# Layer 1's cross attention: scores in five rotating PSUM banks, one bank for the turned probabilities, a loop over 20 batches

## The reference, cut to what matters

```python
B, N, C = x1.shape              # 128, 32, 128
M = x2.shape[1]                 # 257
H, D = (NUM_HEADS, HEAD_DIM)    # 16, 8
q = (x1 @ Wq.T).reshape(B, N, H, D).transpose(0, 2, 1, 3)
k = (x2 @ Wk.T).reshape(B, M, H, D).transpose(0, 2, 1, 3)
v = (x2 @ Wv.T).reshape(B, M, H, D).transpose(0, 2, 1, 3)
q = _layernorm(q, ln_g, ln_b)
k = _layernorm(k, ln_g, ln_b)
q = q * SCALE
attn = jnp.einsum('bhnd,bhmd->bhnm', q, k)
attn = jax.nn.softmax(attn, axis=-1)
out = jnp.einsum('bhnm,bhmd->bhnd', attn, v)
out = out.transpose(0, 2, 1, 3).reshape(B, N, C)
return out @ Wp.T + bp
```

## Time and profile before

| | us |
|---|---|
| median of 3 runs (lowest to highest) | 3743.85 (3743.23 to 3745.98) |
| the profiled execution's own time | 3772.4 |
| its span, first to last instruction | 3770.2 |
| PE busy, share of the span | 2981.6 (79%) |
| DVE busy | 2481.5 (66%) |
| ACT busy | 2041.2 (54%) |
| POOL busy | 1973.8 (52%) |
| first to last `l1x_att_pS` matmul group, start | 802.0 to 1222.4 |

### The profile page before, as it was taken

One profiled execution on the slowest core, in us unless ns is written; L12 is line 12 of the kernel. 1 busy time (PEld: TensorE's weight loads), 2 busy tenths in 40 slices (PEclk: granted clock), 3 DMA queues, 4 the chain that ended last, 5 costly groups with the idle time before them and its releaser, 6 DMA issues. The chain is left out here.

```text
span 3770.2 us, 79125 instructions
## 1 busy us (share of the span) xinstructions
PE 2981.6 (79%) x23619; PEld 2060.2 (55%) x23619; DVE 2481.5 (66%) x6661; ACT 2041.2 (54%) x6345; POOL 1973.8 (52%) x1964
## 2 busy tenths in 40 slices
PE   6989596779999697575999996787862668968967
PEld 5769434446666585453677773333322436735645
DVE  7966676658888573333788885898985123447863
ACT  5545405658888454223677774555530125549954
POOL 5630205767777793053566664888870541117830
PEclk9989798989999798788899998998985778968979
DMA  3300001322222000111111112444431229800000
GB/s 102 91 26 0 6 1 60 101 68 81 79 80 76 8 1 6 59 37 42 41 36 36 36 35 103 135 141 135 146 107 60 31 41 232 199 7 1 2 7 22
DMA packets 142430, 233.64 MB, mean 62 GB/s; under 512 B 28796, under 2 KB 104862, under 8 KB 141575
## 3 DMA queue, kind: packets, MB, share of 16 engines
q1 hardware_dynamic: 134088, 221.61, 20.1%
q0 software_dynamic: 8128, 9.45, 1.4%
HBM read 200.44 MB, written 13.71 MB: 57 GB/s over the span
## 5 line engine op out<-in xcount | busy, mean ns | idle before, releaser
L3208 PE MATMUL l2a_pY<-l2a_hc,ident 128*128 128x512 f32 x512 | 273.4, 673 | 91.3 <-POOL l2a_hc L3127 56.9
L2446 POOL TENSOR_TENSOR l2x_att_prob<-l2x_att_prob,l2x_att_rs 128x1024 f32<-128x1024 f32 x128 | 242.5, 1895 | 148.3 <-DVE l2x_att_rs L2677 148.3
L3097 POOL TENSOR_TENSOR l2a_dbu<-l2a_dx,l2a_BC 128x1024 f32<-128x1024 f32 x128 | 298.7, 2355 | 20.8 <-PE l2a_pY L3208 10.6
L2446 POOL TENSOR_TENSOR l1x_att_prob<-l1x_att_prob,l1x_att_rs 128x1024 f32<-128x1024 f32 x128 | 242.6, 1895 | 106.9 <-DVE l1x_att_rs L2677 106.9
L2634 ACT ACTIVATE l2x_att_prob<-l2x_att_pS,l2x_att_nmx 128x257 f32<-128x257 f32 x512 | 236.4, 475 | 94.5 <-DVE l2x_att_nmx L2672 94.5
L3225 ACT ACTIVATE l2a_pA<-l2a_dl,l2a_A 128x512 f32<-128x512 f32 x256 | 174.7, 690 | 187.7 <-DVE l2a_pH L3331 112.5
L2634 ACT ACTIVATE l1x_att_prob<-l1x_att_pS,l1x_att_nmx 128x257 f32<-128x257 f32 x512 | 236.4, 475 | 72.9 <-DVE l1x_att_nmx L2672 72.8
L3208 PEld LDWEIGHTS l2a_pY<-l2a_hc,ident 128*128 128x128 f32 x512 | 103.6, 211 | 252.8 <-issue 119.4
L2672 DVE TENSOR_REDUCE l1x_att_nmx<-l1x_att_pS 128x1 f32<-128x257 f32 x512 | 182.0, 418 | 89.2 <-PE l1x_att_pS L2545 89.2
L3331 DVE TENSOR_TENSOR_SCAN l2a_pH<-l2a_pA,l2a_dbu 128x512 f32<-128x512 f32 x192 | 224.9, 1217 | 23.5 <-POOL l2a_dbu L3097 12.3
L2672 DVE TENSOR_REDUCE l2x_att_nmx<-l2x_att_pS 128x1 f32<-128x257 f32 x512 | 182.0, 418 | 53.4 <-PE l2x_att_pS L2550 53.4
(11 more groups left out here) (741 smaller groups left out, 9086.4 us busy)
## 6 DMA issues: line engine op xcount, KB each, us to landing
l2a_BC<-l2a_rows SPq DMA_DIRECT2D x128, 512.0 KB, 3.8
l3x_att_ctn<-ctx_n SPq DMA_DIRECT2D x32, 576.0 KB, 12.4
l0x_att_kvs<-ctx_t SPq DMA_DIRECT2D x32, 514.0 KB, 3.6
l1x_k_xin<-ctx_t SPq DMA_DIRECT2D x32, 514.0 KB, 3.5
l1x_att_ctx<-ctx_t SPq DMA_DIRECT2D x128, 128.5 KB, 2.1
l1x_att_kT<-l1x_KA SPq DMA_DIRECT2D x128, 128.5 KB, 2.2
l2x_att_ctx<-ctx_t SPq DMA_DIRECT2D x128, 128.5 KB, 2.1
l3x_att_ctx<-ctx_t SPq DMA_DIRECT2D x32, 514.0 KB, 10.7
```

Of the source, the lines that this page charges most:

```text
L2446: pool.tensor_tensor(p, p, bc(rs[:, b, :], 2, LAST), ALU.mult).then_inc(scaled, 1)
L3097: pool.tensor_tensor(dbu[:, u % 3], dx[:, g % 2], bc(BC[:, u % RING, 0, :], 1, NC), ALU.mult).then_inc(dbu_made, 1)
L3208: last = pe.matmul(pY[c][:, :], env.ident[:, :], hc[:, u % 3, c, :], start=False, stop=n == NS - 1)
```

## The change

For the call with `KA`, `pS` has five banks and `pT` one. Scores of batch t (counted modulo 5) go to banks (4t + j) modulo 5, and so maxima and exponentials read them there. PE's scores wait for a new semaphore `third_read`, counted by the third exponential of the batch before, in place of `p_made`. Both halves of a turn use the one bank: half 0 waits for ACT's copy of the batch before, half 1 for DVE's copy of half 0 of the same batch, and half 1 is issued after `values(n+2)` and no longer before it. PE, ACT and DVE run `run_slots20`, whose loop body is 20 slots (6 passes), since bank numbers must be constants and repeat after five batches and buffers after four. POOL and SP keep `run_slots4`. DVE's and ACT's orders within a slot stay. With `KA=None` everything stays.

```diff
+def run_slots20(eng, slot, units, first, last):
+    low, high = 4, units - 4
+    for n in range(first, low):
+        slot(n, n % 4, n // 4, n % 5)
+    with eng.Fori(0, (high - low) // 20) as i:
+        for c in range(20):
+            slot(20 * i + low + c, c % 4, 5 * i + (low + c) // 4, (low + c) % 5)
+    for n in range(high, units + last):
+        slot(n, n % 4, n // 4, n % 5)
...
-        pS = st.ps("pS", [P, R, 512])
-        pT = [st.ps(f"pT{j}", [P, 512]) for j in range(2)]
+        BANKS = 5 if KA is not None else R
+        pS = st.ps("pS", [P, BANKS, 512])
+        pT = [st.ps(f"pT{j}", [P, 512]) for j in range(2 if KA is None else 1)]
...
+        def bank(t, j):
+            return (R * t + j) % BANKS
+        turns = run_slots4 if KA is None else run_slots20
...
-                    after(pe, p_made, n - 1)
+                    after(pe, p_made if KA is None else third_read, n - 1)
...
-                        last = pe.matmul(pS[:, j, 0:KEYS], ...
+                        last = pe.matmul(pS[:, bank(t, j), 0:KEYS], ...
...
                 def turn(n, b, h):
                     if h == 0:
                         pe.wait_ge(scaled, made(n))
-                        after(pe, t_kept_d, n - 1)
+                        after(pe, t_kept_d if KA is None else t_kept_a, n - 1)
+                    elif KA is None:
+                        after(pe, t_kept_a, n - 1)
                     else:
-                        after(pe, t_kept_a, n - 1)
+                        pe.wait_ge(t_kept_d, made(n))
                     for j in range(R):
-                        last = pe.transpose(pT[h][:, j * P:(j + 1) * P], ...
+                        last = pe.transpose(pT[h % len(pT)][:, j * P:(j + 1) * P], ...
...
                     if inside(n - 1):
                         turn(n - 1, (c - 1) % 4, 0)
-                        turn(n - 1, (c - 1) % 4, 1)
+                        if KA is None:
+                            turn(n - 1, (c - 1) % 4, 1)
...
                     if inside(n + 2):
                         values(n + 2, c, k)
-                run_slots4(pe, slot, B, -2, 3)
+                    if inside(n - 1) and KA is not None:
+                        turn(n - 1, (c - 1) % 4, 1)
+                turns(pe, slot, B, -2, 3)
...
+                        if j == 2 and KA is not None:
+                            last.then_inc(third_read, 1)
                     last.then_inc(p_made, 1)
...
-                    act.activation(probT[:, b % 2, 1, :], pT[1][:, :], ACT.Copy).then_inc(t_kept_a, 1)
+                    act.activation(probT[:, b % 2, 1, :], pT[-1][:, :], ACT.Copy).then_inc(t_kept_a, 1)
...
-                run_slots4(act, slot, B, -2, 3)
+                turns(act, slot, B, -2, 3)
...
-                run_slots4(dve, slot, B, -2, 3)
+                turns(dve, slot, B, -2, 3)
```

More of the change, by code:

```diff
@@ L2533, in last_keys, with scores @@
                     pe.matmul(M, vm[:, :, :].rearrange("p h j -> p (h j)"), wo[:, :]).then_inc(mo_made, 1)
-                def scores(n, c, k):
+                def scores(n, c, k, t):
                     b = (c + 1) % 2
@@ L2541, in scores @@
                         pe.wait_ge(k_landed[b], landed_count(c, k, 1))
-                    after(pe, p_made, n - 1)
+                    after(pe, p_made if KA is None else third_read, n - 1)
                     for j in range(R):
                         r = slice(32 * j, 32 * j + 32)
-                        last = pe.matmul(pS[:, j, 0:KEYS], qb[r, b].rearrange("p h q -> p (h q)"), kT[r, b, 0:KEYS],
+                        last = pe.matmul(pS[:, bank(t, j), 0:KEYS], qb[r, b].rearrange("p h q -> p (h q)"), kT[r, b, 0:KEYS],
                                          start=True, stop=not masked)
@@ L2549, in scores @@
                             r = slice(32 * j, 32 * j + 32)
-                            last = pe.matmul(pS[:, j, 0:KEYS], sel_b[r].rearrange("p h q -> p (h q)"), mask_b[r, :],
+                            last = pe.matmul(pS[:, bank(t, j), 0:KEYS], sel_b[r].rearrange("p h q -> p (h q)"), mask_b[r, :],
                                              start=False, stop=True)
@@ L2584, in output, with slot @@
                               ).then_inc(out_made, 1)
-                def slot(n, c, k):
+                def slot(n, c, k, t=0):
                     if inside(n + 1):
-                        scores(n + 1, c, k)
+                        scores(n + 1, c, k, (t + 1) % 5)
                     if c == 1 and inside(n - 5):
@@ L2633, in exponentials @@
                         act.wait_ge(m_made, made(R * n + j))
-                        last = act.activation(prob[:, b, j, 0:KEYS], pS[:, j, 0:KEYS], ACT.Exp,
+                        last = act.activation(prob[:, b, j, 0:KEYS], pS[:, bank(t, j), 0:KEYS], ACT.Exp,
                                               bias=nmx[:, b, j:j + 1], accum_out=sums[:, b, j:j + 1])
+                        if j == 2 and KA is not None:
+                            last.then_inc(third_read, 1)
                     last.then_inc(p_made, 1)
@@ L2640, in keep_turned, with slot @@
                     after(act, o_made, n - 2)
-                    act.activation(probT[:, b % 2, 1, :], pT[1][:, :], ACT.Copy).then_inc(t_kept_a, 1)
-                def slot(n, c, k):
+                    act.activation(probT[:, b % 2, 1, :], pT[-1][:, :], ACT.Copy).then_inc(t_kept_a, 1)
+                def slot(n, c, k, t=0):
                     if inside(n + 1):
-                        exponentials(n + 1, (c + 1) % 4, k if c < 3 else k + 1)
+                        exponentials(n + 1, (c + 1) % 4, k if c < 3 else k + 1, (t + 1) % 5)
                     if inside(n - 1):
@@ L2667, in _, with maxima @@
                     dve.tensor_copy(mask_b[:, :], mask[:, :]).then_inc(mask_made, 1)
-                def maxima(n, b):
+                def maxima(n, b, t):
                     dve.wait_ge(s_made, made(n))
                     for j in range(R):
-                        dve.tensor_reduce(nmx[:, b, j:j + 1], pS[:, j, 0:KEYS], AX.X, ALU.max, negate=True
+                        dve.tensor_reduce(nmx[:, b, j:j + 1], pS[:, bank(t, j), 0:KEYS], AX.X, ALU.max, negate=True
                                           ).then_inc(m_made, 1)
@@ L2723, in slot @@
                     if inside(n + 1):
-                        maxima(n + 1, (c + 1) % 4)
+                        maxima(n + 1, (c + 1) % 4, (t + 1) % 5)
                     if inside(n + 2) and KA is None:
```

6 lines of the change are left out of this document (3 added, 3 removed).

## The result

The changed kernel takes 3815.97 us (median of four runs, 3811.69 to 3817.17), the kernel before 3743.54 (3739.39 to 3745.98): ratio 1.0195, 95% interval 1.0179 to 1.0211. It is 72.4 us slower, and the forecast was 3813. A second set of runs gave 3809.9 against 3744.77, ratio 1.0190 (1.0128 to 1.0252).

A forecast was written before the change was run, and what follows sets the result against it. A cycle of waits, no full engine, was taken to bound layer 1's cross attention. Cycle 63, ends 2 and loop 4 made 69 us on the median 3743.85: forecast 3813 us, range 3785 to 3850, at 78%.

The forecast's parts named there:

- What bounds: Layer 1's cross attention: no engine is full; a cycle of scores, maxima and exponentials sets the slot at 3.295 us.
- The new cycle: PE's second half waits for DVE's copy behind this slot's maxima, and the next scores follow it: a one-slot cycle.
- Its size: Slot of 3.80 us against 3.295, over 125 slots: 63 us more, bounds 55 to 68.
- The loop: Body of 20 slots: fewer returns gain 0, code fetches at five returns cost 4 us, range 0 to 21.
- The ends: Stage's prologue and epilogue: the second half no longer follows the first at once, 2 us in all.
- Its signs: Slots 3.7 and 3.9 us; transposes wait for DVE about 125 times, 80 us or more; scores' old wait gone.
- Kernel after against profile before: Profiled execution before took 3772.4 us, 28.5 above the median, carried over whole; its successor would take 3841.
- one sign of being wrong: In the stage's loop, every twentieth slot long by more than 1 us would show the forecast wrong.
- Faster: DVE's copy ends before PE reaches its wait at about T+2.5, so PE bounds: 3712 us; 7%.
- The clock: PE's busy share drops to about 79% and the stage's clock falls: +142, about 3892 us; 6%.
- Hard stalls at the returns: Four landings at each of the long loop's five returns, 40 us instead of 4: 3850 us; 6%.

The follow-up runs named there:

- the run bank by bank: Kernel before with DVE's maxima waiting for each score bank by itself, by semaphores on the first three score matmuls, instead of for the fourth: ratio 0.9965 to before.
- the copy between the maxima: Kernel after with DVE's copy of the first half between its third and fourth maximum and PE's first half directly behind the scores: ratio 1.0051 to before.
- four banks in the better order: Kernel after with DVE's copy between third and fourth maximum, PE's first half behind the scores, four score banks and the old wait for p_made: ratio 1.0103.

## Why the prediction was right, point by point

- *What bounds.* The cycle of scores, maxima and exponentials: borne out by the run bank by bank, where 0.07 less in one link shortened the slot by 0.064.
- *The new cycle.* The mechanism is as forecast, and so is its place: PE's second half waits for a copy that stands behind the maxima of this slot's scores. One turn bank alone keeps the loss; moving copy and first half removes most of it.
- *Its size.* Forecast 3.80, measured without returns 3.762. Scores to maximum 0.78 and the copy 0.68 were exact. The second half to the next scores takes 0.59, where I had 0.62 with the gap at 0, and the wait's end to its matmul 0.05 instead of 0.09: 0.07 too much together. From maxima to copy it is 1.54 in plain slots as forecast, but in the slot with the output 1.84 instead of 1.74. The rows of that slot (T = 1009.90):

```profile
1009.90 0.72 PE L2565 MATMUL l1x_att_pS<-l1x_att_kT,l1x_att_qb 32*128 32x257 f32 x8
...
1010.70 0.64 PE L2596 MATMUL l1x_att_pO<-l1x_att_probT,l1x_att_v 128*32 128x128 f32 x16
...
1011.60 0.39 PE L2605 MATMUL l1x_att_pO<-l1x_att_mt,l1x_att_pbd 128*128 128x128 f32 x2
...
1012.10 0.29 DVE L2739 TENSOR_TENSOR l1x_att_own<-l1x_att_pO,m 128x128 f32<-128x128 f32 x1
...
1012.52 0.68 DVE L2726 COPY l1x_att_probT<-l1x_att_pT 128x512 f32<-128x512 f32 x1
```

  PE's attend is 0.16 later than before (T+0.80), as ACT's copy holds it; I had that, with PE's slack as its cover. But in this slot DVE's own_head waits for the output behind it (1011.60+0.39 = 1011.99, own_head at 1012.10), and own_head is on the cycle. The slack that I counted was PE's, the late work was wanted by DVE. It is 0.1 in one slot of four, 3 us, and the error against the two above left 56.1 over 120 slots where the forecast had 60.6.
- *The loop.* Forecast 4 of 0 to 21 us, measured 7.1 over the same slots. The reason was half right: code has to be fetched at the return, but ACT's, not PE's, and PE's slack doesn't cover it: late exponentials make the third of them late, for which the next scores wait. The 7.1 is against no loop. Against the loop of four (454.5 over 120 slots) the term is 4.1, just the forecast's 4, and that is luck: late code that was put at too little, less a gain from fewer returns that was put at nothing. It was wrong that fewer returns gain 0: the return of the loop of four costs 0.09 in the changed order (3.73 against 3.64) and gains 0.09 in the old one (3.22 against 3.31). Why a return shifts the scores by 0.09 is open. In the changed kernel no loop at all takes 451.5, so the loop of four costs 3.0.
- *The ends.* Beyond the 120 slots the forecast had 2.4 for five more slots of the cycle and 2 for the ends; slots 0 to 3 and 124 to 126 give 2.0, and the last scores to the next norm's transposes 2.9 (20.6 to 23.5). The sum of the stage: 69 forecast, 68.1 measured. It is this close because errors cancel: the cycle was 4.5 too much, the loop 3.1 too little.
- *Its signs.* Met: scores that no longer wait for ACT but at the start and the returns, transposes that wait for DVE's copy, a clock of 1.00, slots of 3.64 and 3.84 to 3.95. The wait was to be some 0.7 us a slot. It is 0.57 in one slot of four, 0.44 on average by the matmuls, as PE gets to it at T+2.48 only in that slot, and at T+2.71 to 2.97 in the three others; 80 us came out only by the weight loads. PE was to be busy 79% and is 84%: the forecast took over its old work of 2.99 a slot, and it is 3.22. And one sign of being wrong was met in part, a slot longer by over 1 us at each return: they are 0.9 to 1.1 longer, and the slot ahead of them 0.1.
- *Kernel after against profile before.* I carried the 28.5 us between profile and median over whole. The median of after came out as forecast, but the profiled execution of after was to take 3841 by that and took 3811.69. Those 28.5 us belonged to one execution.
- *Rivals.* Faster: PE was to reach the wait at T+2.5 and did (values out at T+2.48), with the copy not over until T+3.00. That it would pay if the copy came 0.7 earlier was tested by moving it: the time of before, not 32 us better, since the price of splitting the transposes and the wait for ACT's copy of the second half were missing in that rival as well. The clock: 1.00 at 84% busy, so the Trainium skill's case of a clock that oscillates when a kernel cycles through PSUM banks ("TensorE: Matmul & The Clock Gate", "A second HAM failure mode: psum-queue depth-cycling") didn't arise. Hard stalls at the returns: 1 us each, or 2 where a second slot was long, not 8.

## What to carry to other kernels

When two engines hand a bank back and forth inside one slot, write down for each wait what stands ahead of the releasing instruction on its engine. If that needs something which the waiting engine issued earlier in the same slot, and the waiting engine's next such issue lies behind the wait, the slot is that whole chain, however idle the engines are. A freed wait brings nothing until the next chain is shorter too: the fifth bank was worth 0 in one order and 25.8 us in the other, and against the kernel before neither order won anything. Before a loop body is multiplied, ask which engine has the smallest room for code.

## What the runs showed of the hardware that I had not expected

- A loop body of 20 slots is fetched anew on ACT at each return (27 packets on queue 14 against 2), which makes a slot 1.1 to 1.4 us longer in the order of before and 0.9 to 1.1 in that of after. On PE it is not (no long slot, 5 packets on queue 8), though PE's and PEld's rows are some eight times as many as ACT's.
- A loop's return shifts the next waiting matmul by 0.09 us, to the earlier side in one order and to the later in another.
- Eight transposes in two groups of four cost PE 0.16 to 0.24 us of busy time a slot more than in one (3.15 in the copy between the maxima, 3.23 there with four banks, 2.99 before). A weight load behind the scores of 32 rows sits idle 0.33 us, whether it is attend's (before) or a transpose's (four banks in the better order); 0.20 behind attend, 0.17 from transposes to attend. The 0.51 in the kernel with the copy between the maxima is 0.33 and a wait.
- The scores' four products of 32 rows each end within some 0.07 us of each other, by DVE's start in the run bank by bank, though together they take 0.72.
